# Attention of the next chunk between the feed-forward's matmuls, with a two-chunk arena and two shared PSUM banks

## What is computed

```
q = k = v = heads(x)
a  = softmax(mask(q k^T)) v                     # |key - query| <= 256
x1 = ln(x + a)
y  = ln(x1 + relu(x1 @ W1) @ W2)                # W1 [1024,4096], W2 [4096,1024]
u  = layernorm(x + y)
top2 = top_k(softmax(u @ Wg.T + bg), 2), weights renormalised
moe = sum over the 2 experts e of weight_e * (silu(gate_e) * up_e) @ w2_e.T
out = layernorm(u + moe)
```

## Time and profile before

| | us |
|---|---|
| median of 3 runs | 1339.57 |
| lowest and highest of them | 1324.42, 1465.69 |
| the profiled execution, its own time | 1325.35 |
| its span, first to last instruction | 1324.3 |

### The profile page before, as it was taken

One profiled execution on the slowest core, in us unless ns is written; L12 is line 12 of the kernel. 1 busy time (PEld: TensorE's weight loads), 2 busy tenths in 40 slices (PEclk: granted clock), 3 DMA queues, 4 the chain that ended last, 5 costly groups with the idle time before them and its releaser, 6 DMA issues.

```text
span 1324.3 us, 20006 instructions; the slowest of 8 cores (1291.1 to 1324.3 us)
## 1 busy us (share of the span) xinstructions
PE 1066.6 (81%) x6985; PEld 575.2 (43%) x6985; DVE 523.8 (40%) x1140; ACT 428.5 (32%) x581; POOL 328.9 (25%) x488
## 2 busy tenths in 40 slices
PE   4766666798998998999899802999999999995910
PEld 2333333343443444444444301756656656653500
DVE  2476758430453154416423640222222222222775
ACT  5767676432124313421441111111112112110126
POOL 1124213132133314332331221101101011006335
PEclk9757666799998999999999955999999999997965
DMA  9998795499539703941694179989889889805317
GB/s 187 233 169 128 128 144 93 81 169 223 209 80 154 132 33 84 177 90 32 131 171 97 64 146 179 160 167 187 156 179 177 165 170 177 180 32 154 94 40 270
DMA packets 102622, 186.82 MB, mean 141 GB/s; under 512 B 44881, under 2 KB 45009, under 8 KB 99952
## 3 DMA queue, kind: packets, MB, share of 16 engines
q0 software_dynamic: 46288, 126.01, 55.8%
q1 hardware_dynamic: 56224, 59.42, 15.5%
HBM read 251.85 MB, written 37.75 MB: 219 GB/s over the span
## 4 chain that ended last, share of the span: by engine, by line
PE 65%; DMA 9%; DVE 9%; issue 8%; ACT 4%; POOL 3%; DVEq 0%; SPq 0%; POOLq 0%; ACTq 0%
PE pz L553 14%; PE ph L528 12%; PE pg L792 11%; PE pu L792 11%; PE pob L827 10%; DMA wa<-W1p 4%; PE pv L366 3%; PE ps L327 3%; DMA vt<-x0v 2%; ACT wa L341 2%; DMA a<-xs 2%; POOL wa L770 1%; ACT ub L602 1%; DVE tmp L382 1%; DVE wa L355 1%
## 5 line engine op out<-in xcount | busy, mean ns | idle before, releaser
L528 PE MATMUL ph<-wa 128*128 128x512 bf16 x1024 | 234.0, 387 | 16.6 <-DMA wa<-W1p 11.0
L553 PE MATMUL pz<-wa 128*128 128x512 bf16 x1024 | 228.0, 381 | 0.0
L341 ACT ACTIVATE wa<-ps 128x1024 bf16<-128x1024 f32 x160 | 159.3, 1024 | 63.9 <-PE ps L327 62.8
L792 PE MATMUL pg<-wa 128*128 128x320 bf16 x1024 | 165.8, 304 | 13.0 <-issue 10.3
L792 PE MATMUL pu<-wa 128*128 128x320 bf16 x1024 | 164.6, 304 | 2.1 <-issue 2.0
L528 PEld LDWEIGHTS ph<-wa 128*128 128x128 bf16 x1024 | 99.0, 99 | 141.7 <-issue 33.9
L807 DVE TENSOR_TENSOR a<-sg,pu 128x320 bf16<-128x320 bf16 x128 | 62.3, 487 | 223.2 <-ACT sg L803 214.5
L553 PEld LDWEIGHTS pz<-wa 128*128 128x128 bf16 x1024 | 98.7, 98 | 113.9 <-issue 1.6
L803 ACT ACTIVATE sg<-pg 128x320 bf16<-128x320 f32 x128 | 55.9, 437 | 258.8 <-PE pu L792 228.9
L827 PE MATMUL pob<-wa,a 128*128 128x512 bf16 x640 | 139.5, 379 | 0.0
L534 ACT ACTIVATE wa<-ph,b1s 128x512 bf16<-128x512 f32 x128 | 87.9, 686 | 156.5 <-PE ph L528 147.0
(11 more groups left out here) (98 smaller groups left out, 821.3 us busy)
## 6 DMA issues: line engine op xcount, KB each, us to landing
wa<-W1p POOLq DMA_DIRECT2D x128, 256.0 KB
wa<-w1tt POOLq DMA_DIRECT2D x64, 512.0 KB, 10.0
wa<-w2r POOLq DMA_DIRECT2D x16, 1024.0 KB, 15.3
xs<-uT SPq DMA_DIRECT2D x4, 2560.0 KB, 41.1
os<-osb SPq DMA_DIRECT2D x40, 256.0 KB, 3.7
vt<-x0v POOLq DMA_DIRECT2D x32, 260.0 KB
x0s<-x SPq DMA_DIRECT2D x16, 512.0 KB, 25.1
wa<-x0f POOLq DMA_DIRECT2D x32, 256.0 KB
```

Source lines behind the costliest of these rows:

```text
L341: exp_done[s] = self.smark(nc.scalar.activation(self.wa[:, H_AT + 1024 * slot:H_AT + 1024 * slot + 1024], self.ps[s % 2][:], AF.Exp, bias= ...
L528: ins = nc.tensor.matmul(ph[:], self.cols(at + 128 * kc, 128), self.cols(YT_AT + CT * kc, CT), start=(kc == 0), stop=(kc == FC - 1))
L553: ins = nc.tensor.matmul(self.pz[nb][:], self.cols(H_AT + CT * jc + 128 * j, 128), self.cols(W2_AT + 1024 * jc + 512 * nb, 512), start=(jc ...
L792: ins = nc.tensor.matmul(ps[:, 0:n], self.cols(E1_AT[buf] + 2048 * g + kc * 256 + hu * 128, 128), self.cols(XT_AT + FC * CAP * xb + CAP * ...
```

## The change

- **Order.** `phase_attention` becomes a generator `attention(c)` that gives up control after each unit: 40 unit steps for a chunk, then 3 more, 43 in all. Chunk 0's attention runs alone. Attention of chunk c+1 is stepped from inside chunk c's feed-forward: after each of the 64 groups a function `seam` does the steps that are due, then `spread`. For chunk 0 they are due from the first group on, for later chunks from group 11 to group 46 (`ATTN_FROM`, `ATTN_TO`). Before chunk 0's feed-forward there is a loop that runs `norm1`'s tasks, with one attention step for each turn.
- **PSUM.** `ps` and `pv` keep their 6 banks throughout. All else (W1 groups, W2 groups, transposes, logits, counts) shares two banks `pf[0]`, `pf[1]`. `acc` is the bank that accumulates; groups of W1 and 32-matmul runs of W2 alternate between the two. A transpose (now two halves of 4 matmuls, in `turn`), the logits and the counts use the other bank and are copied out by ScalarE; the next user of that bank waits for the copy.
- **SBUF.** One arena `wa` holds everything; float32 rows are kept for 8 tiles (`XC_AT`) instead of 16. A finished tile `u` is stored to DRAM (`us`), after which SP waits for the store and loads the tile 8 further on into its place (`normal`). The experts' phase reads all of `u` back (`u_load`, 8.4 MB). `evac` of a chunk's first head pair pumps tasks until the loads of the chunk's tiles are issued, and waits for them. `NW1` goes from 6 to 4, the exponentials' ring from 10 to 8, and there is one `ub` instead of two.
- **Loads.** W2's four loads are issued in chunk 0's attention, at iterations 1, 3, 5 and 7; the first four W1 blocks at iterations 0 to 3. Seven of expert 0's ten weight blocks (7.3 MB) are issued on GpSimd's queue just ahead of the last chunk, two at the start of its W2 part, one at its end.
- **Pumping.** `norm1` now takes in the cast and the transposes (7 steps, first queue, `LAGF` = 4, two tasks at a time). `norm2` has 14 steps. `LAG` is 7, and up to three tasks take a step after each of the first 20 W1 groups, two elsewhere.

```diff
-LAG = 4
+LAG = 7
+LAGF = 4
...
-RING = 2 * NU
-W2_AT = 0
-W1_AT = 32768
-NW1 = 6
+RING = 8
+NW1 = 4
...
+ATTN_FROM = 10
+ATTN_TO = 46
...
+        queue, lag, n = (self.bgf, LAGF, 2) if self.bgf else (self.bg, LAG, n)
         ahead = 0
-        for task in list(self.bg)[:n]:
+        for task in list(queue)[:n]:
             if len(task) >= ahead:
                 task.popleft()()
+            ahead = len(task) + lag
...
+    def soft(self, i, u):
...
+        last = i - 1 if u >= 3 else i - 2
+        if last >= 0:
+            self.wait("scalar", self.sT, self.pv_done[last])
...
+    def values(self, i, j):
...
+        if j == 3:
+            self.pv_done[i] = self.tmark(ins)
+            self.evac(i)
+            if i + 3 < CH * NP:
+                self.wait("gpsimd", self.sT, self.pv_done[i])
+                self.v_load(i + 3)
+    def evac(self, i):
...
+        if p == 0:
+            while any(4 * c + j not in self.x_tok for j in range(4)):
+                self.spread(2)
+            self.waitd("vector", [self.x_tok[4 * c + j] for j in range(4)])
...
+    def attention(self, c):
+        for i in range(NP * c, NP * c + NP):
+            for u in range(NU):
+                self.scores(i, u)
+                if i % NP and u < 3:
+                    self.values(i - 1, u)
+                    if u == 2:
+                        self.values(i - 1, 3)
+                self.soft(i, u)
+                if u == NU - 1:
+                    if i + 3 < CH * NP:
+                        self.wait("gpsimd", self.sT, self.qk_done[NU * i + u])
+                        self.k_load(i + 3)
+                    if c == 0 and i % 2 == 1:
+                        self.w2_load(i // 2)
+                    if c == 0 and i in (2, 4):
+                        for j in range(2):
+                            self.x_load(2 + i + j)
+                    if c == 0 and i < NW1:
+                        self.w1_load(i)
+                yield
+        for j in range(4):
+            self.values(i, j)
+            if j % 2:
+                yield
+        for j in range(4):
+            self.norm1(4 * c + j)
+        yield
...
+    def turn(self, src, half, ready, dst):
+        nc = self.nc
+        b = 1 - self.acc
+        self.wait("tensor", self.sS, ready)
+        self.wait("tensor", *self.pf_free[b])
+        for k in range(4):
+            ins = nc.tensor.matmul(self.pf[b][:, 128 * k:128 * k + 128],
+                                   self.cols(src + 512 * half + 128 * k, 128), self.idb[:],
+                                   start=True, stop=True)
+        tm = self.tmark(ins)
+        self.wait("scalar", self.sT, tm)
+        m = self.smark(nc.scalar.activation(
+            dst, bass.AP(self.pf[b], 0, [[512, 128], [128, 4], [1, 128]]), AF.Copy, bias=0.0, scale=1.0))
+        self.pf_free[b] = (self.sS, m)
+        return tm, m
+    def small_out(self, b, dst, ins):
+        tm = self.tmark(ins)
+        self.wait("scalar", self.sT, tm)
+        m = self.smark(self.nc.scalar.activation(dst, self.pf[b][:, 0:8], AF.Copy, bias=0.0, scale=1.0))
+        self.pf_free[b] = (self.sS, m)
+        return m
...
     def phase_ffn(self, ahead):
...
+            def seam(n):
+                nonlocal gone, slot
+                slot += 1
+                if steps is not None and slot > start:
+                    want = left * min(slot - start, ATTN_TO - start) // (ATTN_TO - start)
+                    while gone < want:
+                        gone += 1
+                        next(steps, None)
+                self.spread(n)
+            left = self.left if c == 0 else NP * NU + 3
...
-                ph = self.ph[k % 3]
-                self.wait("tensor", self.sS, ph_free[k % 3])
+                b = self.acc = 1 - self.acc
+                ph = self.pf[b]
+                self.wait("tensor", *self.pf_free[b])
...
+                seam(3 if m < 20 else 2)
-                self.w_early = self.w_part(0, range(5))
+                self.w_tok += self.w_part(0, range(FC - 1, FC + 1))
...
+            for _ in ahead or ():
+                pass
+            ahead = self.attention(c + 2) if c + 2 < CH else None
+            if c == CH - 2:
+                self.w_early()
         self.wait("gpsimd", self.sT, tm)
-        self.w_late = self.w_part(0, range(5, FC + 2))
+        self.w_tok += self.w_part(0, range(FC + 1, FC + 2))
...
+        def normal():
...
+            self.wait("sync", self.sV, st[1])
+            self.u_tok[t] = self.qdma(bass.AP(self.us.tensor, 128 * t * D, [[D, 128], [1, D]]), x)
+            if t + 8 < NT:
+                self.waitd("sync", self.u_tok[t])
+                self.wait("sync", self.sS, st[2])
+                self.x_load(t + 8)
...
+            for _ in self.attention(0):
+                pass
             self.xr_load(0)
-            self.phase_ffn()
+            ahead = self.attention(1)
+            self.left = NP * NU + 3
+            while self.bgf:
+                if self.left > 3:
+                    self.left -= 1
+                    next(ahead)
...
+        for t in range(NT - 8, NT):
+            self.waitd("gpsimd", self.u_tok[t])
         wtoks[1] = self.ws_load(1)
         stored = []
         xt = {0: (0, first)}
         self.last_split()
```

564 lines of the change are left out of this document (247 added, 317 removed).

## The result

The changed kernel takes 1.1194 times as long as the one before, 95% interval [1.1052, 1.1335]: median 1494.48 us (1479.15 to 1591.09) against 1337.11 us. Its profiled execution took 1479.15 us, 107 us more than the 1372 forecast and 44 us above the range. The direction was right, the size was not: one of the terms, the wait for a tile's bf16 copy, was kept at 5 us a chunk and took 26 to 29.

A forecast was written before the change was run, and what follows sets the result against it. PE's order was taken to set the feed-forward and the experts. Stages 126 + 137 + 189 + 189 + 158 = 799 us against 757, so + 42, + 5 for the experts: 1325.35 + 47 = 1372 us, range 1285 to 1435.

The forecast's parts named there:

- 5 us a chunk: Feed-forward: PE's wait for a tile's bf16 copy, 16.5 us in 12 waits before, stays at 5 us a chunk.
- The shared banks: W1 parts: PE waits for ScalarE's copies out of the shared banks, 1.05 us a use, 1.4 with an exponential ahead.
- Attention between groups: Attention steps placed between feed-forward groups cost PE 0.74 us each; 43 steps are 32 us a chunk.
- The wait for x: W1 part, group 17: evac forces the pump and PE waits for the x load, 9 us, bounds 0 and 15.
- The clock: Rival, chance 0.12: the clock falls in W1 groups mixed with attention, adding 54 us, near 1425 us.
- under 0.9 between groups: Sign against the forecast: it is wrong if the clock between groups is under 0.9.
- The start: Before the first W1 group: loads in queue order, values behind W2, put that group at 126 us.
- Chunk 0: Chunk 0's feed-forward: matmuls 110.7, 29 remaining attention steps 21.5, half transposes 2.4, waits 2; 137 us.
- Chunk 3: Last chunk's feed-forward: W1 part 100 us, W2 part 58 as today; 158 us.
- 14 + 4: Chunk 3's W1 part: 14 us waiting behind expert weights (bounds 5 and 22), 4 us for the smaller W1 ring.
- Behind it: After the feed-forward: tail stays 66 us; u_load delays the experts' first transposed rows by 5 us, bounds 0 and 25.
- The sum: Whole kernel: feed-forward ends at 799 us where today 757; 42 + 5 = 47 us more, 1372 us; chance 0.48.

The follow-up runs named there:

- e1: Changed kernel with two bf16 copies of a tile (ub) instead of one; 1419.5 us, ratio 1.0694.
- e5: Changed kernel with scores in one double bank from chunk 1's attention on, the two freed banks taking transposes, logits and counts; 1438.8 us, ratio 1.084.
- e4: Changed kernel with the next chunk's attention issued in one lump at one seam, not spread; 1560.47 us profiled, ratio 1.1809.
- e8: Changed kernel with the changes of e1, e5 and e2 together, W1 slots 5 for 4 and exponentials' ring 7 for 8; 1337.5 us, ratio 1.0136.
- e2: Changed kernel with W2 in 16 pieces over two chunks' attention, expert weights issued later, u read back in four parts; 1451.69 us profiled, ratio 1.101.
- e12: e8 with W2 not loaded, VectorE writing a constant; only the first 275 us read: chunk 0's W2 part ends at 257.9 us (274.8).
- e11: e8 with one empty step between copy and transposes in each tile's task; ratio 1.0149.

## Why the prediction was right or wrong

**One buffer for two: the step that failed.** The diff had it, and the prediction kept "5 us a chunk" for the copy from the earlier trace rows, "that stays". It took 28.9, 29.4 and 25.5 us in the W1 parts of chunks 1 to 3, and the one buffer cost 66 us in all, by e1. A scatter's landing had a row in the trace before ("786.72 2.75 DMA xs<-ub,rowi" in the tail), and in the W1 parts of the changed kernel the time from the issue of a tile's second scatter to the copy's release is 3.7 to 6.6 us (nine in the chain). The working should have asked who reads `ub` last, how many steps after the copy, and how many steps a seam now runs.

**The shared banks: right.** Forecast 16 uses of 1.05 to 1.4 us a chunk; the W1 part of chunk 1 shows 9.0, 4.2 and 3.7 us in 15 waits, 1.13 each. e5 gives 47 us for the whole. The forecast had this term near 20 us for each of chunks 1 and 2 and 17 for chunk 3, 56 in all. One of its inputs, 0.2 us for a copy of 8 columns, stood in none of the rows named for it; the changed kernel has it at 0.17.

**Attention between groups: right in size.** 0.74 us a step forecast; the difference of e4 and the changed kernel gives 20 us for 26 steps in the W1 part (19.2 forecast) and 10 for 17 in the W2 part (12.6).

**The wait for x: right place, wrong releaser.** 9 us a chunk were forecast, at group 17, where `evac` forces the tasks on. TensorE does stop there in chunks 1 and 2, behind the 17th group, but for the copy; this is chunk 1:

```profile
353.07 0.17 PE L708 MATMUL pf<-macc,ones 128*128 128x8 bf16 x1
363.29 0.59 PE L495 MATMUL pf<-idb,wa 128*128 128x128 bf16 x4 [10.06 <-ACT wa L657]
```

VectorE then waits for x, 17.9 us in two waits, and TensorE shows none of it. With two buffers (e1) the stop is still 5.91 us. So the 9 us for x never came: an error of the other sign, and without it the forecast would have been 18 us lower.

**The clock: under-weighted.** It was a rival at 0.12, worth 54 us. The granted clock is 0.80 to 0.85 in the W1 parts of chunks 1 to 3, in 20-us stretches down to 0.57 (of 1.0, 2.4 GHz), after groups with a wait of 1 to 10 us between them. The W1 matmuls are busy 266.2 us where the earlier trace rows have 234.0: 32 us. It goes with the waits, but not with the copy's alone: the second copy brings the 266.2 to 255.9, and with all repairs (e8) they are still 257.1, 23 us above the kernel before. The forecast named "under 0.9 between groups" as a sign against it. The Trainium skill's "TensorE: Matmul & The Clock Gate", section on PSUM-queue depth-cycling, describes such a loss from micro-idles between groups; the trace agrees in kind. I had set that rule aside because of the quiet feed-forward before.

**The start: 12 us short, wrong releaser.** 138 for 126. The waits are for keys (x0f, 61.8 us), not for vt. Moving W2 behind brought the start to 124 (e2), so W2's load ahead of the keys was the right mechanism; e12 doesn't decide it.

**Chunk 0: right in the sum**, 139 for 137. The working counts 29 remaining steps where 43 less 17 are 26, 2 us too much.

**Chunk 3: 42 us short.** W1p's wait is 21.4 us for the 14 + 4 of the forecast; the copies took 20 us more than the 5 given; the W2 part takes 66 us for 58, and 58 was a misreading, since it took 60 before. The rest is mostly the clock of 0.80.

**Behind it: 15 us short.** The experts took 388 us for 368 before; 5 were given. The bounds (0 and 25) held. The mechanism named, transposed rows behind `u_load`, was right: 36.7 us of issuing on SyncE ahead of them come through to TensorE as a wait of 18.9 us.

**The sum.** Excess over the forecast by stage: 12 + 2 + 20 + 19 + 42 to the end of the feed-forward, 96; with the experts' 15, less 1 in the tail and about 3 in rounding and output, 107. Of the stages behind the start, the one missed term and its clock carry most.

**Where the gain went.** With its causes repaired the change still only comes within 1 to 2% of the kernel before. By stages of e8_ring: the first two attentions and the first feed-forward take 275 us for 259, and W2's load costs 17 by e12. Chunks 1 and 2, each with the attention of the next chunk, take 181 and 178 us for 129 + 62 and 123 + 63, a gain of 10 and 8. Chunk 3 takes 137 for 124. In chunk 1 that attention stood at 62 us and adds 30 when spread (by e4 and the changed kernel), which would be a gain of 32. The waits of TensorE in its W1 part, in e8_ring, take it back:

```profile
PE ps L497 <- ACT wa L665: 13.9, 4, 5.9
PE ps L352 <- ACT wa L367: 5.0, 4, 1.5
PE pv L390 <- DVE wa L379: 2.1, 1, 2.1
PE pf L581 <- DMA wa<-W1p: 0.9, 2, 0.5
```

22 us of 32, and e11 shows that moving the first of them by one seam gives rise to others. The busy times say it without e4. Before, TensorE idled 21 us in the attention and 8 in the feed-forward of this chunk, 29 in all; in e8_ring it idles 28. The idle time of the attention was not filled but moved to the W1 part, and the gain of 10 is nearly all busy time, 152.4 us for 161.5. The W1 matmuls took part of that gain back too, at a clock of 0.90 for 0.95: 67 us for 59 in this chunk. The 13 us of chunk 3 were not taken apart.

No version here beats the kernel before. The nearest, e8_ring, is at 1.0136 [1.0033, 1.0238].

## What to carry to other kernels

Where a diff takes a buffer away, price it by its last reader (here scatters 4 to 7 us from landing) and by the number of steps between that and the next writer in the new order; a quiet row of the old order says nothing. When work is interleaved, its chains over other engines meet the matmuls' in-order queue, so price each hand-over between engines inside one seam, and expect a clock loss on top where they come through as gaps. Look also for places that force a queue on (here `evac`): they put steps back to back, whatever distance is set between them.

## What the runs showed of the hardware that was not expected

- The granted clock of chunk 1's W1 part went from 0.82 to 0.96 when one kind of gap (four in the part, up to 10.1 us, 28.9 in sum) was shortened to 5.9 us at most and 11.6 in sum, the matmuls being the same and the bank waits 18.0 us for 16.9. In chunks 2 and 3 it went only from 0.85 to 0.91 and from 0.80 to 0.86.
- A scatter of a 128 x 1024 bf16 tile takes about 1.0 us of GpSimd to issue. From the issue of a tile's second one to the release of what waits for it are 3.7 to 6.6 us in the W1 parts (nine in the chain of the changed kernel).
- SyncE's first DMA transpose of an expert's rows holds the engine for 45.4 us in the kernel before and 53.5 us in the changed one, behind 8.4 MB of its own loads; the six after it hold it for 15 to 19 us each. Issuing the four loads of those 8.4 MB held it for 36.7 us.
- Moving W2's loads by tens of microseconds changed where the start waits and not when chunk 0's W1 part ends (212.6 and 211.6 us): up to there the DMA engines are 0.87 to 0.95 busy.
